# The first stage of a four-layer kernel: two tiles normalised and projected first, six behind, no barrier

## What is computed

```python
x = L0_attn_x                                   # (4, 256, 512)
xn = _layernorm(x, axis=-1)                     # (x - mean) / sqrt(var + 1e-5)
x = x + _L0_attn_ref(xn, wq, wk, wv, wo) + _L0_ffn_ref(xn, ...)
...                                             # three more layers of this form
```

## Time and profile before

| | us |
|---|---|
| three runs of the kernel | 1501.34, 1503.41, 1503.43 |
| their median | 1503.41 |
| the profiled execution | 1503.67 |
| its span, first to last instruction | 1501.4 |

### The profile page before, as it was taken

How to read it: one execution, slowest core, us unless ns; L and a number is a source line. 1 busy time by engine, 2 the same in 40 slices (tenths; PEclk the granted TensorE clock), 3 DMA queues, 4 the chain that set the end, 5 groups by cost and what they waited for, 6 DMA issues and landing times.

```text
span 1501.4 us, 25866 instructions
## 1 busy us (share of the span) xinstructions
PE 1395.1 (93%) x9284; PEld 1209.9 (81%) x9284; DVE 1006.8 (67%) x1821; ACT 710.6 (47%) x1856; POOL 464.4 (31%) x360
## 2 busy tenths in 40 slices
PE   3999999799999796989999999999999999948998
PEld 2878888567777575879999999999999999837887
DVE  7666666679999734466667766677666776664554
ACT  3666666622222222246556665556555565422332
POOL 5211111122321741425344442525243444124000
PEclk9999999999999897899999999999999999979999
DMA  6101020232230001111212121101102020010000
GB/s 210 30 1 30 2 72 6 80 106 84 84 119 0 22 1 45 36 36 29 71 29 70 28 70 28 62 9 41 56 28 70 28 70 28 1 63 8 15 14 28
DMA packets 39685, 67.90 MB, mean 45 GB/s; under 512 B 4940, under 2 KB 13799, under 8 KB 39618
## 3 DMA queue, kind: packets, MB, share of 16 engines
q1 hardware_dynamic: 37522, 65.69, 13.7%
q10 hardware_dynamic: 2096, 1.33, 0.3%
HBM read 60.68 MB, written 2.13 MB: 42 GB/s over the span
## 4 chain that ended last, share of the span: by engine, by line
PE 87%; DVE 7%; ACT 2%; issue 1%; DMA 1%; POOL 0%; SPq 0%; DVEq 0%; POOLq 0%; ACTq 0%
PE PS L348 21%; PE PS L350 20%; PE PS L349 20%; PE PS L1568 3%; PE PS L1866 3%; PE PS L1852 2%; PE PS L1851 2%; PE PS L1853 2%; PE PS L1501 2%; PE PS L1587 2%; PE PS L1549 1%; PE PS L1521 1%; DVE ln_xn L935 1%; PE PS L1842 1%; PE PS L1583 1%
## 5 line engine op out<-in xcount | busy, mean ns | idle before, releaser
L348 PE MATMUL PS<-XNH,E_WL 128*128 128x256 f32 x768 | 214.9, 280 | 0.8 <-DVEq L343 0.8
L350 PE MATMUL PS<-XNH,E_WH 128*128 128x256 f32 x768 | 214.7, 280 | 0.0
L349 PE MATMUL PS<-XNL,E_WH 128*128 128x256 f32 x768 | 214.0, 279 | 0.0
L553 POOL TENSOR_TENSOR E_sw<-E_sw,rope2s 128x1024 f32<-128x1024 f32 x64 | 104.5, 1633 | 274.2 <-ACT E_sw L605 274.2
L1277 DVE TENSOR_REDUCE E_nb<-PS 128x4 f32<-128x512 f32 x64 | 61.3, 958 | 178.6 <-PE PS L1853 178.6
L605 ACT ACTIVATE E_sw<-PS 64x256 f32<-64x256 f32 (+1 forms) x128 | 89.5, 700 | 120.7 <-PE PS L350 119.2
L348 PEld LDWEIGHTS PS<-XNH,E_WL 128*128 128x128 f32 x768 | 144.5, 188 | 2.4 <-DVEq L343 1.2
L349 PEld LDWEIGHTS PS<-XNL,E_WH 128*128 128x128 f32 x768 | 144.5, 188 | 1.2
L350 PEld LDWEIGHTS PS<-XNH,E_WH 128*128 128x128 f32 x768 | 144.3, 188 | 0.0
L463 POOL TENSOR_TENSOR E_WL<-raw,E_WH 128x512 fp32r<-128x512 f32 x80 | 110.0, 1404 | 106.7 <-ACT E_WH L605 106.2
L801 ACT ACTIVATE E_p<-PS,E_nb 128x128 f32<-128x128 f32 (+1 forms) x256 | 104.3, 420 | 34.5 <-DVE E_nb L1277 34.5
(11 more groups left out here) (272 smaller groups left out, 4036.3 us busy)
## 6 DMA issues: line engine op xcount, KB each, us to landing
raw<-in_w SPq DMA_DIRECT2D x104, 256.0 KB, 2.7
words<-in_words SPq DMA_DIRECT2D x11, 768.0 KB, 4.2
wo<-in_wo SPq DMA_DIRECT2D x32, 256.0 KB, 3.7
zb<-z_scratch SPq DMA_DIRECT2D x11, 384.0 KB, 4.9
scb<-in_scales SPq DMA_DIRECT2D x11, 384.0 KB, 5.5
X<-in_x SPq DMA_DIRECT2D x8, 256.0 KB, 6.0
SGH<-XNH SPq DMA_DIRECT2D x8, 256.0 KB, 2.7
SGL<-XNL SPq DMA_DIRECT2D x8, 256.0 KB, 2.8
```

The source lines that it names most:

```text
L348: nc.tensor.matmul(o, sl, mh, start=first, stop=False, **shared)
L349: nc.tensor.matmul(o, sh, ml, start=False, stop=False, **shared)
L350: return nc.tensor.matmul(o, sh, mh, start=False, stop=last, **shared)
L553: nc.gpsimd.tensor_tensor(E_sw[:, heads, :], E_sw[:, heads, :], rope2s[:, :].unsqueeze(1).broadcast_to([P, heads.stop - heads.start, SEQ]) ...
```

## The change

**Loads.** SP issues x tiles 0 and 1, weight units 0 to 7, x tiles 2 to 7, weight units 8 to 11, and then six constants on a semaphore of their own (`late_in`). Units 5 to 11 have places of their own in buffers that attention uses later (`A_p`, `A_pT`, `OT0`). ACT's queue loads three constants. The layer norm's buffers no longer share their place with `A_p`.

**Order.** Tiles 0 and 1 go through statistics, scale, transposes and rests alone; DVE scales them. Units 0 to 4 follow, with the statistics of tiles 2 to 7 between them on DVE; ACT scales tiles 2 to 7 (`scale_rows`, with a negated shift that DVE makes) and copies their high parts; DVE makes their rests last. The rests of weight units 5 and 7 move from POOL to DVE. The first scores wait for all eight tiles. The two first pieces of v are projected in slot 0, behind the first scores of t = 1, and copied by DVE, not ACT. The zero points are made in slots 4, 5 and 6.

**Removed.** The barrier, and `SGH`, `SGL` and their 16 copies: the projections read `XNH` and `XNL`. Units come in the order q tile 0, q tile 1, k tile 0, k tile 1, the first five into two banks in turn. Waits on counts are renumbered to match.

```diff
                 A_p = sb(st, "A_p", [P, 12, P])
                 A_pT = sb(st, "A_pT", [P, 12, P])
                 OT0 = sb(st, "OT0", [P, KT, SEQ])
                 OT0s = [OT0, raw[:, 3:5, :].rearrange("p r (k t) -> p (r k) t", t=SEQ)]
+                parts0 = [raw[:, u, :] for u in range(RAW)]
+                for t, n in ((A_p, 3), (A_pT, 3), (OT0, 1)):
+                    flat = t[:, :, :].rearrange("p n t -> p (n t)")
...
-            for tt in range(TT):
-                sp.dma_start(X[:, tt, :], d["x"][tt]).then_inc(x_in[tt // 2], 16)
+            def load_x(tiles):
+                for tt in tiles:
+                    sp.dma_start(X[:, tt, :], d["x"][tt]).then_inc(x_in[tt // 2], 16)
+
+            def load0(units):
+                for u in units:
+                    sp.dma_start(parts0[u], d["w0"][u]).then_inc(raw_in[u] if u < RAW else w0_in[u - RAW], 16)
+
+            load_x(range(2))
+            load0(range(8))
+            load_x(range(2, TT))
+            load0(range(8, 12))
+            for t, name in [(identb, "identb"), (mask_ts, "mask_ts"), (mask01, "mask01"), (shift_k, "shift_k"), (rope2c, "rope2c"), (rope2s, "rope2s")]:
+                sp.dma_start(t[tuple(slice(None) for _ in t.shape)], d[name]).then_inc(late_in, 16)

...
-            for u in range(12):
-                load_unit(U_QKV0 + u, u % RAW, d["w0"][u])
-
-            def stage(b):
-                for tl in range(2):
-                    if not isinstance(b, int) or b >= 1:
-                        sp.wait_ge(a["vps"], b * 4 + (tl - 1))
-                    else:
-                        ln_wait(sp, 0, "lo", tl + 1)
-                    tok, at = bass.ds(b * SEQ + tl * P, P), slice(tl * P, (tl + 1) * P)
-                    sp.dma_start(f32(SGH[:, :, at]), f32(XNH[:, :, tok])).then_inc(a[f"stage{tl}"], 16)
-                    sp.dma_start(f32(SGL[:, :, at]), f32(XNL[:, :, tok])).then_inc(a[f"stage{tl}"], 16)
...
-            pool.wait_ge(const_in, 16 * 9)
+                    if u < RAW:
+                        rest(u, WQH[:, u, :], WQL[:, u, :], u)
+                    else:
+                        pool.wait_ge(w0_hi, u - RAW + 1)
+                        nc.gpsimd.tensor_tensor(WQL[:, u, :], parts0[u], f32(WQH[:, u, :]), ALU.subtract).then_inc(w0_lo, 1)
+
+            rests0((0, 1, 2, 3, 4, 6))
...
+            rests0(range(8, 12))
...
+            for t, name in [(ident, "ident"), (rope0c, "rope0c"), (rope0s, "rope0s")]:
                 act.dma_start(t[tuple(slice(None) for _ in t.shape)], d[name]).then_inc(const_in, 16)
...
+            ready = [prepared(-1, g) for g in FIRST]
+            split0((0,))
+            roots(0, slice(0, 2))
+            split0((1, 2, 3))
+            take_rows(0)
+            split0((4,))
+            take_rows(1)
+            split0((5, 6, 7))
+            take_stacks(ready[0])
+            take_stacks(ready[1])
+            split0((8, 9))
+            take_stacks(ready[2])
+            roots(1, slice(2, TT))
+            scale_rows(2)
+            scale_rows(3)
+            split0((10, 11))
+            take_rows(2)
+            scale_rows(4)
+            take_rows(3)
+            scale_rows(5)
+            take_stacks(ready[3])
+            for tt in range(4, TT):
+                take_rows(tt)
+                if tt + 2 < TT:
+                    scale_rows(tt + 2)
             for b in range(NB):
                 attend(b)
             take_first(NB * G0)
...
+                    if t == 0:
+                        dve.wait_ge(a["init"], 2)
+                        for tl in range(2):
+                            take_values((None, 0, 0, tl, None), 2, 4, tl)
...
+                    if b == 0 and 4 <= g < 7:
+                        zeros_plus_one(g - 4)
...
-            zeros_plus_one(0)
-            turn_heads(prepared(-1, FIRST[0]))
-            for g in FIRST:
-                unit = prepared(-1, g)
-                if FIRST[1] <= g <= FIRST[2]:
-                    zeros_plus_one(g - FIRST[0])
-                stack_heads(unit)
-                if g < G0 - 1:
-                    turn_heads(prepared(-1, g + 1))
...
+            ready = [prepared(-1, g) for g in FIRST]
+            statistics0((0, 1))
+            scales0(0, 0, 2)
+            scale_rows0(0)
+            scale_rows0(1)
+            row_rests0(0)
+            row_rests0(1)
+            weight_rest0(5)
+            dve.wait_ge(const_in, 16 * 3)
+            turn_heads(ready[0])
+            weight_rest0(7)
+            stack_heads(ready[0])
+            turn_heads(ready[1], 3)
+            statistics0((2, 3, 4))
+            stack_heads(ready[1])
+            turn_heads(ready[2])
+            statistics0((5, 6, 7))
+            stack_heads(ready[2])
+            turn_heads(ready[3], 3)
+            scales0(1, 2, TT)
+            shifts0(2)
+            stack_heads(ready[3])
+            turn_heads(ready[4])
+            row_rests0(2)
+            stack_heads(ready[4])
+            for tt in range(3, TT):
+                row_rests0(tt)
+            dve.wait_ge(late_in, 16 * 6)
             least(0, 0)
             for b in range(NB):
                 attend(b)
...
-            pe.wait_ge(const_in, 16 * 9)
-            normalise(0)
-            finish(pe, 1)
...
-                if half == 0 and is_k == 0:
-                    pe.wait_ge(a[f"stage{tl}"], b * 32 + 32)
...
+
+            def first_project(unit):
+
+                U, b, half, tl, is_k = unit
+                ln_wait(pe, 0, "lo", tl + 1)
+                if is_k:
+                    pe.wait_ge(w_lo, 5)
+                    pe.wait_ge(w0_lo, 1)
+                    pe.wait_ge(w0_rest, 2)
+                else:
+                    pe.wait_ge(w_lo, 4)
+                after(pe, a["t1"], U - 1)
+                after(pe, a["t2"], U - 1)
+                dense(PS[:, 5 - U % 2 * 2, 0:HALF], is_k, b, half, tl).then_inc(a["proj"], 1)
+
+            def first_values():
+
+                pe.wait_ge(w0_lo, 5)
+                for tl in range(2):
+                    dense(PS[:, 4, tl * HALF:(tl + 1) * HALF], 2, 0, 0, tl, clear=(tl == 0)).then_inc(a["vps"], 1)
...
+                    if t == 0:
+                        first_values()
...
+            ready = [prepared(-1, g) for g in FIRST]
+            pe.wait_ge(const_in, 16 * 3)
+            rows0(0)
+            rows0(1)
+            first_project(ready[0])
+            first_project(ready[1])
+            first_project(ready[2])
+            transposes(ready[0])
+            first_project(ready[3])
+            transposes(ready[1])
+            first_project(ready[4])
+            transposes(ready[2])
+            rows0(2)
+            rows0(3)
+            transposes(ready[3])
+            for tt in range(4, TT):
+                rows0(tt)
+            pe.wait_ge(late_in, 16 * 6)
+            ln_wait(pe, 0, "lo", TT)
             scores(0, 0)
```

More of the change, by code:

```diff
@@ L39, in build_program @@
     E2, R2 = 8, 16
-    U_QKV0, U_W1 = 0, 12
+    U_W1 = RAW
     U_WB2 = U_W1 + KT
@@ L254, in build_program @@
         const_in = sem("const_in")
+        late_in = sem("late_in")
+        w0_in = [sem(f"w0_in{u}") for u in range(12 - RAW)]
+        w0_hi = sem("w0_hi")
+        w0_lo = sem("w0_lo")
+        w0_rest = sem("w0_rest")
+        nb_in = sem("nb_in")
         x_in = [sem(f"x_in{n}") for n in range(TT // 2)]
@@ L651, in ffn_heads @@
                     copy(FWH[p][:, c, :], F_w[:, c, :], f["hi"])
-            def take_values(unit):
-                _, _, half, _, tl = unit
-                ps = PS[:, 3, 0:HALF].rearrange("p (k e j d) -> p k e j d", k=2, e=2, j=4)
-                for e in range(2):
-                    ins = copy(V0[:, tl, 2 * half:2 * half + 2, e, :, e * D0:(e + 1) * D0], ps[:, :, e, :, :])
-                ins.then_inc(a["vcp"], 1)
             def take_stacks(unit):
@@ L951, in add_dense, with statistics0 @@
                 V.tensor_tensor(X[:, tt, :], X[:, tt, :], PS[:, 4 + tt % 3, :], ALU.add).then_inc(ffn_x, 1)
-            for tt in range(TT):
-                if tt % 2 == 0:
-                    dve.wait_ge(x_in[tt // 2], 32)
-                statistics(0, tt)
-            normalise(0)
-            finish(dve, 1)
+            def statistics0(tiles):
+                for tt in tiles:
+                    if tt % 2 == 0:
+                        dve.wait_ge(x_in[tt // 2], 32)
+                    statistics(0, tt)
@@ new lines, in shifts0, with scale_rows0, row_rests0 @@
+            def shifts0(first):
+                B = LN[0]
+                V.scalar_tensor_tensor(B["tmp"][:, first:TT], B["mv"][:, first:TT, 0], -1.0, B["rstd"][:, first:TT], ALU.mult, ALU.mult)\
+                 .then_inc(nb_in, 1)
+            def scale_rows0(tt):
+                B = LN[0]
+                V.tensor_scalar(B["xn"][:, tt, :], X[:, tt, :], B["mv"][:, tt, 0:1], B["rstd"][:, tt:tt + 1], ALU.subtract, ALU.mult)\
+                 .then_inc(ln["xn"], 1)
+            def row_rests0(tt):
```

(15 more changed lines are left out.)

129 lines of the change are left out of this document (61 added, 68 removed).

## The result

The changed kernel takes 1495.97 us (median of 13 runs, 1494.20 to 1502.25) where the kernel before took 1503.25 (13 runs, 1501.28 to 1507.81). The ratio is 0.9955, with a 95% interval from 0.9944 to 0.9966: by it 6.8 us less, between 5.1 and 8.4 (the medians differ by 7.3). The prediction said 1497.0, and 6.5 less. The profiled execution of the changed kernel took 1495.88, span 1493.8 (before 1503.67 and 1501.4).

What follows compares the result with a forecast made beforehand. PE holds the chain nearly throughout, except in the beginning, where DVE bounds until 29.79. 10.0 gained less 1.1 (v), 1.2 (clock) and 1.2 (zero points) gives 6.5, so 1497.0; range 1492.5 to 1501.0.

Steps and rivals of the forecast that it cites:

- First tiles: Beginning: two tiles of x instead of eight; root at 7.9, scaling 10.3, PE's transposes 11.6, first projection 13.9.
- the table load: Ahead of the first root on ACT: costs 1.28 by the profile row; with the skill's drain, later times 1.4 later.
- Five units and tiles 2 to 7: Beginning up to scores: units end at 28.1, constants 29.7, ACT sets the pace, first scores 39.7 instead of 49.75, 10.0 gained.
- v: Slot 0: two first pieces of v take 2.9 of PE, partly filling its waits; net 1.1 given back, bounds 0 and 2.9.
- Clock: Entry to the scores: PE at half clock, part hidden behind ACT in slots 0 and 1; 1.2 given back, bounds 0 and 3.4.
- Zero points: Ends of slots 4, 5 and 6: three groups of 2.0 on DVE; 1.2 given back, bounds 0 and 2.7.
- last rival: Slots 4 to 6: DVE becomes the bound, zero points cost 10.2 and slow stretches 5.1; 7.6 slower, 1511, chance 0.03.
- Slot 2 by 7 to 9 earlier: Sign that the forecast is right: first scores of slot 2 come by 7 to 9 earlier than before.
- Behind 290 us every distance stays: Sign that the forecast is right: behind 290 us, every distance to the kernel before should stay.
- PE stays slow: Rival, entry and slots: clock 3.4 and zero points 2.7 at their bounds, v 1.1; gain 2.8, 1500.6, chance 0.16.
- The slow stretches go: Rival, attention: slow stretches may not follow PE's waits, entry may be at full clock; gain 10.0, 1493.4, chance 0.18.

Runs made afterwards that it cites:

- PE kept busy: Changed kernel, with PE repeating matmuls whose result nothing reads in its waits between 27.3 and 40 us; median 1496.28, ratio 0.9943.
- the last version but one: Changed kernel with all single edits but repeated matmuls, three more edits, and five repeated matmuls ahead of each of tiles 4 to 7; median 1489.86, ratio 0.9914.
- the second trace: Changed kernel run again with nothing edited; median 1499.51 of 9 runs, ratio 0.9957 to the kernel before.

## Why the prediction was right, point by point

**First tiles: right.** Root 7.9 (7.96), scaling 10.3 (10.29), transposes 11.6 (11.68), first projection 13.9 (14.18). That the early start hangs on weight unit 0 is shown by the run with x first: 4.0 later there, 4.0 later at the scores. The other 5.6 of the 9.6 (two tiles first, no barrier, no zero points between the units) no run takes apart; for it speaks that every mark came within 0.8 of its forecast. On the table load the trace went by its own row: 6.67 and 1.28 end at 7.95, and the root starts at 7.96. The drain of the Trainium skill (ScalarE: Activation LUTs, What ACT_TABLE_LOAD costs) does not show.

**Five units and tiles 2 to 7: right.** Eviction 28.1 (27.37), constants 29.7 (29.57), first scores 39.7 (40.15). Two sizes cancelled within ACT's chain: what follows a scaling starts 0.70 behind it, what follows a copy about 0.5, and I took 0.60 for both. The same page of the Trainium skill says that each operand of one value per partition adds about 93 ns to an activation; the scaling has two, and its row of 0.80 beside the copy's 0.60 agrees.

**v: near in size, 1.35 against 1.1, at full clock only.** At full clock, slots 0 and 1 took 11.14 without v (before) and 12.49 with it (PE kept busy); against the 10.91 of the last version but one it is 1.58. With half clock on entry, as in the changed kernel, v cost 2.2 to 2.3 (15.15 against 12.96 and 12.86). That the waits that it was to fill had gone into the slow slot is my reading; no run shows it.

**Clock: the step that was mis-sized, together with v.** I said 1.2, "part hides behind ACT in slots 0 and 1". It cost 2.66 with v in (15.15 against 12.49; 2.13 by the second trace) and 2.05 without (12.96 against 10.91), and next to nothing hid. Slot 0 took 4.45 before, of which only 0.53 were waits: a slow PE of 6.5 us becomes the bound at once. Clock and v together are 4.0 of measured cost where I said 2.3. How that divides depends on which is taken away first (1.35 and 2.66, or 2.3 and 1.7); in the first division nearly all of the miss is the clock's, in the second more of it is v's. With the measured 9.6, 1.35 and 2.66 the prediction's sum would have been 4.4, and with the measured zero points 5.0.

**Zero points: 1.2 said, 0.57 and 0.54 measured.** (The prediction's threshold for its last rival, 2.7 per group, does not follow from its terms: 7.7 less 5.1 leaves 2.6 for three groups above their 1.1 of idle time, so 2.0 per group.) Groups of 1.6 to 2.0 that overrun idle times of 0.78 to 1.32 delayed the minima, but the gaps later in each slot took up more than half.

**Slot 2 by 7 to 9 earlier: wrong** (5.6), by the clock and v. **Behind 290 us every distance stays: wrong in the trace** (6.3, then 5.6, then 7.6), and not by the change: the same program differed from itself by 5.0.

**Rivals.** "PE stays slow" got its clock term nearly right (2.66 of 3.4) and its zero points wrong. "The slow stretches go" came true for one stretch, in slot 9 of the first trace and in slot 5 of the second, but not on entry. The prediction had written that a stretch followed the first of the two waits for DVE's outputs; in the kernel before one followed the second as well, at 111.

**The total: partly luck.** What the terms give is 9.6 - 4.0 - 0.6 = 5.0, just below the measured 5.1 to 8.4. The prediction's terms were 1.5 too good together (clock 1.5, beginning 0.4 and v 0.25 too good, zero points 0.6 too bad). The one stretch fewer in slots 5 and 9, which the forecast left out, gave 1.5 in both traces, so that 6.5 stood there from slot 9 on. Whether it belongs to the change is likely and not shown; nor is what the last few tenths up to 6.8 are. So the forecast was right in its mechanism, and its 6.5 came about by two errors of 1.5 that cancelled.

## What to carry to other kernels

When the beginning of a kernel is made shorter, cost the clock with which PE enters the steady part as its own term, at what PE loses in the slow stretch unless it has real waits there: with the gaps ahead of it filled the clock stayed at 1.00, and without that a start 1.4 earlier was worth 0.3. Before a tuned kernel's term of 1 or 2 us is believed or doubted by the whole time, trace the same program twice, and compare marks near the edit. And ask of every operation put on POOL what DVE does beside it, and what is queued behind it.

## What the runs showed of the hardware that I had not expected

Tiny DVE operations beside POOL's: 0.17 alone, 1.26 and 1.01 beside a rest; a copy of 0.43 took 0.83, and a rest of 0.68 took 1.75. The clock of 1.2 GHz stayed for 5 to 7.5 us behind the first scores in all five traces with v where the change put it and no repeated matmuls, whether the scores began at 39.2 or at 44.2; with PE busy between 27 and 40 it read 1.00 throughout the entry. A wait of 1.7 of PE, at the same place of the same program, had a slow stretch with it in one trace and none in the next. An activation with two operands per partition takes 0.80 where one without takes 0.60. And two traces of one program, with the same instructions, had their slow stretches in different slots and differed by 5.0 us.
